# A convolution, attention and FFN kernel: new homes and a new order for the first phase's stages

## The reference, cut to what matters

```python
x = einsum('oc,bchw->bohw', inv(I - circulant(ricker(width, damp))), x)    # 16 x 128 x 32 x 32
t = to_tokens(x)                                                            # 16 x 1024 x 128
n = layernorm(t)
Q, K, V = elu(n Wq^T) + 1, elu(n Wk^T) + 1, n Wv^T                          # 8 heads of 16
S, z = cumsum(outer(K, V), tokens), cumsum(K, tokens)
t = t + ((Q S) / max(Q z, 1e-6)) Wout^T
n = layernorm(t)
g = (relu(n Wg1^T + b) Wg2^T + b2).mean(tokens)                             # 16 x 8, one gate row a batch
W1m, b1m, W2m, b2m = base + g . task vectors                                # merged weights of each batch
out = layernorm(n + relu(n W1m^T + b1m) W2m^T + b2m) * merged_gain + merged_bias
t = t + out
```

## Time and profile before

| | us |
|---|---|
| median of 3 runs | 847.6 (845.93 to 848.53) |
| the profiled execution | 848.7 |
| its span in the trace | 846.9 |
| TensorE busy in the span | 739.7 (87%) |
| VectorE busy | 742.6 (88%) |
| ScalarE busy | 670.2 (79%) |
| GpSimd busy | 534.6 (63%) |
| first phase | about 27 to 571 |

### The profile page before, as it was taken

One profiled execution on the slowest core, in us unless ns is written; L12 is line 12 of the kernel. 1 busy time (PEld: TensorE's weight loads), 2 busy tenths in 40 slices (PEclk: granted clock), 3 DMA queues, 4 the chain that ended last, 5 costly groups with the idle time before them and its releaser, 6 DMA issues. The chain is left out here.

```text
span 846.9 us, 37199 instructions
## 1 busy us (share of the span) xinstructions
PE 739.7 (87%) x11168; PEld 538.4 (64%) x11168; DVE 742.6 (88%) x2736; ACT 670.2 (79%) x1875; POOL 534.6 (63%) x1009
## 2 busy tenths in 40 slices
PE   1588999999999999999999999968899998899994
PEld 1255666666666666666666666648577777577773
DVE  6587999999999999999999999955788985689894
ACT  1477898999989989998898988844788885688884
POOL 5486888888888888888988988810133342033333
PEclk9888999999999999999999999977999999999998
DMA  2255444454444444544454444410022221122222
GB/s 80 52 126 118 98 111 105 92 117 109 91 111 106 105 105 100 116 106 99 106 111 95 116 100 98 88 33 26 2 77 86 77 74 51 38 64 76 74 87 75
DMA packets 165473, 74.10 MB, mean 87 GB/s; under 512 B 139212, under 2 KB 152687, under 8 KB 165368
## 3 DMA queue, kind: packets, MB, share of 16 engines
q1 hardware_dynamic: 165432, 73.58, 36.0%
HBM read 22.69 MB, written 17.30 MB: 47 GB/s over the span
## 5 line engine op out<-in xcount | busy, mean ns | idle before, releaser
L795 DVE SCALAR_TENSOR_TENSOR scores_lo<-p_a,scores_hi 128x512 f16<-128x512 f32 x256 | 164.0, 682 | 0.0
L698 ACT ACTIVATE scores_hi<-p_a 128x512 f16<-128x512 f32 x256 | 138.5, 600 | 6.4 <-PE p_a L543 6.2
L861 POOL TENSOR_TENSOR stats<-stats,consts 128x1 f32<-128x1 f32 x128 | 78.1, 610 | 75.7 <-DVE stats L745 75.6
L1312 POOL TENSOR_TENSOR ffn_rstd_shift<-ffn_rstd_shift,consts 128x4 f32<-128x4 f32 x32 | 36.7, 1146 | 132.8 <-DVE ffn_rstd_shift L1271 132.8
L886 POOL TENSOR_TENSOR qk_parts<-qk_f,qk_parts 128x128 f16<-128x128 f32 x256 | 104.9, 429 | 0.1
L867 POOL TENSOR_TENSOR stats<-stats,consts 128x1 f32<-128x1 f32 x128 | 89.0, 695 | 18.7 <-DVE stats L751 17.1
L560 PE MATMUL p_o<-v_parts,scores_hi 128*128 128x17 f16 x1024 | 90.2, 171 | 12.1 <-ACT scores_hi L698 6.2
L560 PEld LDWEIGHTS p_o<-v_parts,scores_hi 128*128 128x128 f16 x1024 | 80.4, 96 | 30.0 <-issue 27.6
L1095 PE MATMUL psb<-merged_W_of_batch,h_hi 128*128 128x128 f16 x512 | 94.2, 220 | 4.9 <-DVE h_lo L1249 3.8
L1249 DVE TENSOR_TENSOR h_lo<-h_f,h_hi 128x512 f16<-128x512 f32 x128 | 95.0, 782 | 1.2 <-ACT h_hi L1152 1.2
L1141 ACT ACTIVATE h_f<-psb,merged_b_of_batch 128x512 f32<-128x512 f32 x128 | 87.0, 711 | 11.4 <-PE psb L1076 11.3
(11 more groups left out here) (195 smaller groups left out, 3009.6 us busy)
## 6 DMA issues: line engine op xcount, KB each, us to landing
x_f<-in_x SPq DMA_DIRECT2D x32, 256.0 KB, 2.9
t_rows<-t SPq DMA_DIRECT2D x64, 128.0 KB, 1.9
t_back<-t_rows SPq DMA_DIRECT2D x32, 256.0 KB, 2.6
out<-out_tile SPq DMA_DIRECT2D x32, 256.0 KB, 2.0
tv_share<-in_L_ffn_tv_W SPq DMA_DIRECT2D x32, 128.0 KB, 2.2
qkT_parts<-qk_parts SPq DMA_TRANSPOSE x128, 3.1
base_ffn_weights<-in_L_ffn_W SPq DMA_DIRECT2D x2, 256.0 KB, 4.3
W_hi_lo_rows<-base_parts SPq DMA_DIRECT2D x4, 128.0 KB, 3.8
```

The costliest lines, as they stand in the source:

```text
L698: nc.scalar.activation(ah[:, t % 2, cols], p_a[:, cols], ACT.Relu).then_inc(ahi_ready[eo], 1)
L795: nc.vector.scalar_tensor_tensor(al[:, t % 2, cols], p_a[:, cols], 0.0, ah[:, t % 2, cols], ALU.max, ALU.subtract).then_inc(alo_ready[eo], 1)
```

## The change

1. **State by heads.** `state` writes for each head a 64 x 17 and a 64 x 16 product into the head's own block of the bank, 16 matmuls in place of 8, even heads in partitions 0 to 63, odd heads in 64 to 127. The bank is cleared once at the start, so the unwanted quarters stay zero. `read_state` and its mask product are gone: `state_hi` is a copy out of PSUM on ScalarE, `state_lo` a subtraction on VectorE.
2. **z.** `shift2` (VectorE, one element in each partition) makes -mean x rstd, and `normalise` is an activation with scale and bias on ScalarE. z is split before it is turned: `z_hi` (ScalarE, from SBUF) and `z_lo` (GpSimd) write `z_parts`, and a DMA on SP's queue transposes both parts into zT. The TensorE transpose of z is gone; `gate` uses the PSUM bank of `turn_out`.
3. **q and k.** `q_hi` goes from ScalarE to GpSimd, beside `k_hi`.
4. **Order.** The tables are new, with skews up to 11 in place of 8 (`scores` of a tile one or two slots later, its two ScalarE halves on either side of a slot's end); the loop is surrounded by two unrolled batches on either side.

```diff
-TENSOR_ORDER = [("conv", 0), ("project", 0), ("turn_out", 5), ("gate", 8), ("values", 4), ("turn_z", 7),
-                ("state", 2), ("out_project", 5), ("scores", 2)]
+TENSOR_ORDER = [("conv", 1), ("turn_out", 7), ("values", 6), ("out_project", 7), ("state", 4), ("gate", 11),
+                ("project", 1), ("scores", 4)]
...
-                        at_least(pe, sm_ready, (TILES - 1) * b + t)
-                        for a in range(NP):
-                            kk = pk[:, t % 4, 1, 2 * a:2 * a + 2, :].rearrange("p h c -> p (h c)")
-                            mm(sbank[:, a, :], kk, vp[:, t, 2 * a:2 * a + 2, 0:VW],
-                               start=(t == 0 and a == 0), stop=False, skip_group_check=True)
...
+                        at_least(pe, sp_ready, (TILES - 1) * b + t)
+                        for h in range(NH):
+                            e, kk = h % 2, pk[:, t % 4, 1, h, :]
+                            o = sbank[64 * e:64 * e + 64, h // 2, e * VW:(e + 1) * VW]
+                            mm(o, kk, vp[:, t, h, 0:VW], start=(t == 0 and h < 2), stop=False, skip_group_check=True)
+                        for h in range(NH):
+                            e, kk = h % 2, pk[:, t % 4, 1, h, :]
+                            o = sbank[64 * e:64 * e + 64, h // 2, e * VW:e * VW + DH]
+                            last = mm(o, kk, vp[:, t, h, VW:VW + DH], start=False, stop=True, skip_group_check=True)
                         last.then_inc(su_done, 1)
...
+                    def turn_z(b, t):
+                        n = TILES * b + t
+                        parts = n + 1 if isinstance(n, int) else sp.to_reg(n + 1)
+                        sp.wait_ge(ones_set, 1)
+                        sp.wait_ge(zlo_ready, parts)
+                        sp.dma_start_transpose(zz[:, :, bass.ds(n * P, P)],
+                                               zp[:, t % 4, :, :].rearrange("p w c -> p (w c)"))\
+                            .then_inc(z_turned[t % 4], 16)
...
+                        act.wait_ge(su_done, m + 1)
+                        at_least(act, av_done, TILES * b + t - 2)
+                        nc.scalar.activation(sp2[:, t % 4, 0, :, :], sbank, ACT.Copy).then_inc(sh_ready, 1)
...
+                        act.wait_ge(shift_ready, n + 1)
+                        at_least(act, zlo_ready, n - 1)
+                        nc.scalar.activation(z_[:, t % 2, :], yt[:, t, :], ACT.Identity, bias=st2[:, t % 4, 10:11],
+                                             scale=st2[:, t % 4, 8:9]).then_inc(z_ready, 1)
...
+                        nc.scalar.activation(zp[:, t % 4, 0, :], z_[:, t % 2, :], ACT.Copy).then_inc(zhi_ready, 1)
...
+                        nc.vector.scalar_tensor_tensor(st2[:, t % 4, 10:11], st2[:, t % 4, 6:7], -1.0,
+                                                       st2[:, t % 4, 8:9], ALU.mult, ALU.mult).then_inc(shift_ready, 1)
...
+                        dve.wait_ge(sh_ready, m + 1)
+                        nc.vector.tensor_tensor(sp2[:, t % 4, 1, :, :], sbank, sp2[:, t % 4, 0, :, :], ALU.subtract)\
+                            .then_inc(sp_ready, 1)
...
+                    def qk_hi(w, done):
+                        def stage_(b, t):
...
+                            for i in range(2):
+                                at_least(pool, sc_done[i], used)
+                            src = qk[:, t % 4, w * C:(w + 1) * C].rearrange("p (h i) -> p h i", i=DH)
+                            dst = pk[:, t % 4, w, :, :].rearrange("p h (a b i) -> p h a b i", a=2, b=2)
+                            dst = dst[:, :, :, 0, :] if w == 0 else dst[:, :, 0, :, :]
+                            nc.gpsimd.tensor_copy(dst, src.unsqueeze(2).broadcast_to([P, NH, 2, DH])).then_inc(done, 1)
...
+                        pool.wait_ge(zhi_ready, n + 1)
+                        nc.gpsimd.tensor_tensor(zp[:, t % 4, 1, :], z_[:, t % 2, :], zp[:, t % 4, 0, :], ALU.subtract)\
+                            .then_inc(zlo_ready, 1)
```

More of the change, by code:

```diff
@@ L38 @@
 BIG = -1.0e30
-TENSOR_ORDER = [("conv", 0), ("project", 0), ("turn_out", 5), ("gate", 8), ("values", 4), ("turn_z", 7),
-                ("state", 2), ("out_project", 5), ("scores", 2)]
[L44 to L51, removed]
+TENSOR_ORDER = [("conv", 1), ("turn_out", 7), ("values", 6), ("out_project", 7), ("state", 4), ("gate", 11),
+                ("project", 1), ("scores", 4)]
+SCALAR_ORDER = [("copy_out", 7), ("scores_hi_0", 5), ("exp_qk", 2), ("z_hi", 9), ("split_x", 0), ("tv_hi", 0),
+                ("relu_qk", 2), ("state_hi", 4), ("gate_relu", 11), ("read_t1", 7), ("v_hi", 2), ("normalise", 8),
+                ("scores_hi_1", 4)]
+VECTOR_ORDER = [("eps1", 2), ("v_lo", 3), ("stats1", 1), ("mean_var2", 8), ("scores_lo_1", 5), ("eps2", 8),
+                ("scores_lo_0", 5), ("tv_lo", 0), ("denominator", 6), ("mean_var1", 1), ("invert", 6), ("shift2", 8),
+                ("make_qk", 2), ("state_lo", 4), ("divide", 6), ("stats2", 7)]
+GPSIMD_ORDER = [("qk_lo", 4), ("rsqrt2", 9), ("z_lo", 10), ("split_x", 1), ("k_hi", 3), ("q_hi", 3), ("rsqrt1", 2)]
+SYNC_ORDER = [("turn_z", 11), ("load_x", 4), ("load_tv", 3), ("store", 8), ("turn", 3)]
 FFN_TENSOR_ORDER = [("up_0", 0), ("up_3", 0), ("up_1", 0), ("down_0", 1), ("down_1", 1), ("down_2", 1),
@@ L454, in _ @@
                                 .then_inc(base_placed, 16)
-                    with sp.Fori(1, B - 1) as b:
+                    batch(stages, 1)
+                    with sp.Fori(2, B - 1) as b:
                         batch(stages, b)
-                    batch(no_loads, B - 1)
-                    batch(no_loads, B, new=False)
+                    for b in range(B - 1, B + 2):
+                        batch(stages, b)
                     for pair in range(TILES // 2):
@@ L464, in _ @@
                     mm = nc.tensor.matmul
[L468 to L469 removed]
+                    banks = [{"conv": (bn1,), "out_project": (t1_ready,)},
+                             {"turn_out": (oT_ready,), "gate": (gate_ready,)}]
                     def bank_read(stage, n):
@@ L914, in _ @@
                     run(pool, GPSIMD_ORDER, {"rsqrt1": rsqrt1, "qk_lo": qk_lo,
-                        "state_hi": state_hi, "state_lo": state_lo, "split_x": split_x,
-                        "rsqrt2": rsqrt2, "k_hi": k_hi})
+                        "split_x": split_x,
+                        "rsqrt2": rsqrt2, "q_hi": qk_hi(0, qhi_ready), "k_hi": qk_hi(1, khi_ready), "z_lo": z_lo})
         with ExitStack() as pb:
```

162 lines of the change are left out of this document (60 added, 102 removed).

## The result

The change makes the kernel slower: 861.7 us median of 4 runs (858.2 to 865.2) beside 847.5 us of the kernel before, ratio 1.0169, 95% interval 1.0109 to 1.0229. The forecast was 833.8 us, with a range of 816 to 858. The profiled execution took 858.25 us, its span is 856.2 us.

What follows compares the result with a forecast made beforehand. VectorE was taken as the bound before the change, ScalarE after it. The profiled 848.7 us less 20.8 for 16 batches plus 7 for the ends gave 834.9, or 833.8 us against the median; range 816 to 858.

Steps and rivals of the forecast that it cites:

- VectorE 29.1 us a batch: VectorE's busy time per batch of eight tiles was to fall by 3.0, from 32.1 to 29.1 us.
- the ruler: Batch length read from 15 tv split starts, 56.8 to 515.8 us: 32.79 us a batch, 4.10 a tile.
- ScalarE 30.4 to 31.3: ScalarE's busy time per batch was to rise from 29.6 to between 30.4 and 31.3 us, making it the fullest engine.
- 31.5 us a batch from ScalarE as the fullest engine: Steady batch, the middle of 31.1 and 32.0 us: 1.3 less than now, times 16 = -20.8 us.
- GpSimd 28.6: GpSimd's busy time per batch was to rise by 0.5, from 28.1 to 28.6 us, with q_hi at 0.39.
- Rival 1: GpSimd in series with make_qk becomes the bound: 856 us at q_hi 0.49; chance 0.17.
- TensorE, 16 state matmuls at 0.03: The state's 16 small matmuls on TensorE were priced at 0.03 us each, 0.48 a tile in place of 0.21.
- rival 2: TensorE's narrow weight loads cost 0.07 us each in the state, 33.9 us a batch, 872 us; chance 0.10.
- SyncE's DMAs at nothing: Eight more turning DMAs a batch on SP's queue were to cost nothing, 0 to +3 us at the phase's end.
- The ends, +7: Start and end of the phase, with more light slots and z's last DMA: +7 us (3 to 12).
- Rival 3: The move buys nothing: four engines interlock, the batch stays at 32.8 us, only the ends are paid, 855 us; chance 0.13.

Runs made afterwards that it cites:

- the best version: The changed kernel with z's turning DMA one slot earlier in SyncE's order and divide ahead of state_lo on VectorE: 827.7 us, 0.9765 of before.
- the copies: One more 128x128 copy a tile on ScalarE ahead of z_hi, added to the best version: 835.2 us, 0.9849 of the kernel before the change.

## Why the prediction was wrong, by its steps

- **VectorE 29.1 us a batch**: right in the sum, 290.73/320 x 32.41 = 29.4, by two errors that cancel. With the ruler put right the forecast would be 31.7 - 3.0 = 28.7, and shift2 was mis-sized: 0.07 us taken, 0.25 in step on average between 200 and 320 us.
- **ScalarE 30.4 to 31.3**: right at the lower end, 30.4 by the same sum; z's normalise was mis-sized: 0.34 taken, 0.47 in step (307.66 to 308.13) and 0.38 at its shortest between 200 and 440 us. z_hi was not, 0.20 taken and 0.19 in step (306.24 to 306.43):

```profile
306.24 0.30 ACT L715 ACTIVATE z_parts<-z 128x128 f16<-128x128 f32 x1
306.43 0.47 ACT L677 ACTIVATE relu_qk<-p_in,stats 128x256 f32<-128x256 f32 x1
...
307.66 0.50 ACT L707 ACTIVATE z<-t,stats 128x128 f32<-128x128 f32 x1
308.13 0.60 ACT L692 ACTIVATE scores_hi<-p_a 128x512 f16<-128x512 f32 x1
```

- **31.5 us a batch from ScalarE as the fullest engine**: the number came (31.4 undisturbed with z's slot mended, 31.9 on average), but by luck, since ScalarE is not what holds it, and from a base of 32.36 it is a gain of 0.9 us a batch, or 0.5 on average, not 1.3. In the best version ScalarE was 97.6% busy and took in the copies all the same. Records of neighbours overlap by about 0.1 us (0.30 long, 0.20 in step), so a busy share hides gaps; the prediction knew the overlap and took it off prices, but not off the share that it divided by.
- **GpSimd 28.6**: 26.2 us. q_hi costs as k_hi (all 158 casts are 0.397 to 0.403 us long), and the two powers got shorter, 0.55 us each on average where they had been 0.61 and 0.70, which is 1.7 us a batch; of the rest, 0.4 is the ruler's:

```profile
L882 POOL CAST qk_parts<-qk_f 128x256 f16<-128x256 f32 x158 | 58.7, 400 | 43.9 <-issue 43.9
L868 POOL TENSOR_TENSOR stats<-stats,consts 128x1 f32<-128x1 f32 x79 | 43.5, 551 | 10.0 <-DVE stats L762 9.5
L862 POOL TENSOR_TENSOR stats<-stats,consts 128x1 f32<-128x1 f32 x79 | 43.5, 550 | 7.3 <-DVE stats L756 5.9
```

  Rival 1 did not come, though make_qk still stretches to 0.89 us beside x_lo (310.81 to 311.48 on GpSimd), and shift2 is held to 0.38 beside z_lo (from 310.42), as that rival allowed. The tile on GpSimd and on VectorE:

```profile
310.42 0.43 POOL L898 TENSOR_TENSOR z_parts<-z,z_parts 128x128 f16<-128x128 f32 x1
310.81 0.67 POOL L907 TENSOR_TENSOR x_lo<-x_f,x_hi 128x256 f16<-128x256 f32 x1
```
```profile
310.49 0.38 DVE L785 SCALAR_TENSOR_TENSOR stats<-stats 128x1 f32<-128x1 f32 x1
310.87 0.89 DVE L779 SCALAR_TENSOR_TENSOR qk_f<-exp_qk,relu_qk 128x256 f32<-128x256 f32 x1
```

- **TensorE, 16 state matmuls at 0.03**: right. L533 starts at 302.49, gate's L606 at 302.92: 0.43 us, 0.027 each (0.36 us in the run with z's turn earlier), so rival 2 falls. The loads are recorded 0.11 us long and overlap. The Trainium skill ("TensorE: Matmul & The Clock Gate", LDWEIGHTS) gives 53 ns for a load of 64 columns; this trace does not agree, since a load and its matmul together take half of that in step:

```profile
302.49 0.30 PE L533 MATMUL p_s<-v_parts,qk_parts 128*64 128x17 f16 x8
302.63 0.28 PE L537 MATMUL p_s<-v_parts,qk_parts 128*64 128x16 f16 x8
302.92 0.23 PE L606 MATMUL p_m<-zT_hi_lo,gate_hi 128*128 x1
```
```profile
L537 PEld LDWEIGHTS p_s<-v_parts,qk_parts 128*64 128x64 f16 x420 | 11.2, 113 | 0.0
```

- **SyncE's DMAs at nothing, because "z's turn comes a tile ahead of its reader"**: this is the step that failed. The sum of the holds was right (1.24 and 1.17 us, and 0.36 for a load or store, of 4.05). The distance was wrong: turn_z and gate both have 11, and what stands ahead of turn_z is a turn that waits for qk_lo of the same tile time, so the DMA was issued 2.5 us before gate's start in the tile above, of which its landing takes 2.3. The sentence after it looked whether q and k wait for z, never whether z waits for q and k. Changing this one number was worth 22.9 us.
- **The ends, +7**: from the last exp to the last gate it is 23.6 us after and 23.3 before; with the 1.0 at the start, 1.3 in place of 7. This term was mis-sized: the end with nine slots is as long as it was with seven.
- **Rival 3**, 855 us, had the outcome (the batch stays) but its cause, an interlock among four engines, was not it. No case had the clock of the early batches: they were priced like all others, and cost 8.5 of the 9.3 us in place of a gain.

With z's slot mended the kernel runs in 838.8, within the forecast's own range (820 to 845), and that too is partly luck. In its profile the first exp and the last are 9.5 us closer than before, where the batches were to give 20.8, and the rest of the span is 1.0 us shorter, where the ends were to cost 7.

## What to carry to other kernels

When a step moves to a queue served in program order, follow its operand through that queue: what stands ahead of it, which semaphore that one waits for, and when the reader comes. Here the data was ready 4.6 us before its DMA could be issued, and one number in a table turned 1.7% slower into 0.9% faster. Read a period from entries of the steady stretch alone, and take a busy share that is made of overlapping records as an upper bound of an engine's load. Before calling an engine the bound, give it a little more work and see what shows.

## What was unexpected

- A turning DMA holds the queue for about as long with 2 blocks of 128x128 (1.17 us) as with 8 (1.24 us), and lands in 2.3 against 3.1 us.
- With z's short waits in the early batches TensorE's granted clock was 0.84 and 0.81 in two stretches of 40 us, and 0.91 and 1.00 with them gone; together that was worth 11 us in four batches. It does not take z's wait: with the extra subtraction on VectorE, which has none, the second stretch is at 0.87.
- In the four runs with only z's slot or gate's moved to mend it, the clock fell once in three batches, with TensorE busier than before (305 of 320 us). In the first of them it fell at 221.5, 317.1 and 412.6 us, for 3.4 us each, and such a batch took 1.3 us more. A stretch of 4 us around one of them reads 0.57, a little over half:

```profile
221.00:225.00 4.00, 4.00 (x51) 2.22 (x51) 2.44 (x14) 2.63 (x9) 2.83 (x7) 0.57 0.43 82
```

  Two us ahead of each TensorE had waited 0.70 us for divide (until 219.28 for the first), but that wait comes in every batch (251.88, 283.35) and only each third was followed by a fall. With divide ahead, TensorE busy for 311 of 320 us, none came between 180 and 500 us. What sets them off is open.
